# A graph network kernel: aggregation by groups of four tiles, counting by tile pairs, both with their outer loops written out

## The reference

```
out = segment_sum(hx[src] * al[:, :, None], dst, num_segments=n)   # self loops are among the edges
x = relu(out + b + x)          # first round; the second adds x and the original rows, with no relu
```

## Time and profile before

| | |
|---|---|
| median of 3 runs | 4544.77 us (4540.06 to 4547.14) |
| profiled execution | 4547.42 us, of which the span is 4545.9 us |
| busy in the span: PE, DVE | 2962.5 us, 2218.4 us |
| busy in the span: POOL, ACT | 977.4 us, 370.0 us |
| counting | about 231 to 837 us of the span |
| aggregation, round 0 and 1 | about 1254 to 1782 us, and 2124 to 2596 us |

### The profile page before, as it was taken

How to read it: one execution, slowest core, us unless ns; L and a number is a source line. 1 busy time by engine, 2 the same in 40 slices (tenths; PEclk the granted TensorE clock), 3 DMA queues, 4 the chain that set the end, 5 groups by cost and what they waited for, 6 DMA issues and landing times. The chain is left out here.

```text
span 4545.9 us, 68833 instructions
## 1 busy us (share of the span) xinstructions
PE 2962.5 (65%) x16813; PEld 1910.2 (42%) x16939; DVE 2218.4 (49%) x5486; ACT 370.0 (8%) x793; POOL 977.4 (21%) x985
## 2 busy tenths in 40 slices
PE   1467677563066765602777628923999999989476
PEld 1133333352054454501555426712656565656345
DVE  7465656587356664712444420065444444444463
ACT  0211111100000000000000012212000000000131
POOL 0000000076367700566774020020000000000000
PEclk9888989876589898756999959966999999999797
DMA  1200000253134411623553153223121212121101
GB/s 60 69 29 36 32 32 32 103 194 118 30 107 119 116 27 54 204 65 111 140 140 93 59 202 125 101 65 135 57 94 57 93 57 93 57 94 57 37 0 40
DMA packets 206513, 378.78 MB, mean 83 GB/s; under 512 B 35807, under 2 KB 155344, under 8 KB 203222
## 3 DMA queue, kind: packets, MB, share of 16 engines
q1 hardware_dynamic: 120090, 188.27, 11.9%
q0 software_dynamic: 50384, 139.33, 10.9%
q10 hardware_dynamic: 35968, 50.35, 3.2%
HBM read 270.37 MB, written 108.29 MB: 83 GB/s over the span
## 5 line engine op out<-in xcount | busy, mean ns | idle before, releaser
L1850 PE MATMUL hop_wide<-hop_hs,counts 128*128 128x512 bf16 x3000 | 990.9, 381 | 35.0 <-DMA hop_hs<-hop_parts 35.0
L1851 PE MATMUL hop_narrow<-hop_hs,counts 128*128 128x256 bf16 x3125 | 855.8, 274 | 170.6 <-DMA hop_hs<-hop_parts 155.5
L653 POOL DMA_INDIRECT gat_ring<-hx_rows,src_i x784 | 793.4, 1012 | 339.3 <-issue 211.2
L1850 PEld LDWEIGHTS hop_wide<-hop_hs,counts 128*128 (+1 forms) x3125 | 307.1, 98 | 577.9 <-issue 215.5
L888 PE MATMUL cnt_acc<-cnt_oh_src,cnt_oh_dst 128*128 x1764 | 407.0, 367 | 137.3 <-issue 71.5
L1241 PE MATMUL agg_acc<-agg_msg,agg_oh 128*128 x880 | 278.3, 444 | 126.4 <-DVE agg_oh L1180 125.9
L888 PEld LDWEIGHTS cnt_acc<-cnt_oh_src,cnt_oh_dst 128*128 x1764 | 180.5, 102 | 350.8 <-issue 292.6
L1851 PEld LDWEIGHTS hop_narrow<-hop_hs,counts 128*128 (+1 forms) x3125 | 307.2, 98 | 36.4
L1823 DVE TENSOR_SCALAR hop_h<-hop_narrow,all_dis 128x256 f32<-128x256 f32 x125 | 60.5, 484 | 527.2 <-PE hop_narrow L1851 527.2
L1241 PE MATMUL agg_acc<-gat_ring,agg_oh 128*128 x880 | 258.4, 417 | 89.0 <-DVE agg_oh L1177 89.0
L848 DVE TENSOR_SCALAR cnt_oh_src<-cnt_number,cnt_column 128x1600 f16 x441 | 277.6, 629 | 0.0
(11 more groups left out here) (408 smaller groups left out, 3557.6 us busy)
## 6 DMA issues: line engine op xcount, KB each, us to landing
look_part<-src_low SPq DMA_DIRECT2D x28, 896.0 KB, 4.9
hop_hs<-hop_parts POOLq DMA_DIRECT2D x25, 960.0 KB, 8.1
hop_parts<-hop_parts SPq DMA_DIRECT2D x125, 192.0 KB, 1.9
count_rows<-cnt_out SPq DMA_DIRECT2D x50, 400.0 KB, 2.4
counts<-count_rows ACTq DMA_DIRECT2D x5, 4000.0 KB, 35.2
exp_w<-in_L_ffn_w SPq DMA_DIRECT2D x16, 1024.0 KB
hop_acc<-x_gcn SPq DMA_DIRECT2D x125, 128.0 KB, 2.0
x_gcn<-hop_acc SPq DMA_DIRECT2D x125, 128.0 KB, 1.8
```

Of the source, the lines that this page charges most:

```text
L653: pool.indirect_dma_start(out=self.ring[:, t % RING, :], out_offset=None, in_=self.g.hx_rows, in_offset=bass.IndirectOffsetOnAxis(ap=self. ...
L1850: pe.matmul(wide[i][:, :], count, hs[:, t, 0:2 * D], start=(t == 0), stop=(t == NB - 1))
L1851: mm = pe.matmul(narrow[i][:, 0:D], count, hs[:, t, 2 * D:3 * D], start=(t == 0), stop=(t == NB - 1))
```

## The change

Counting goes by pairs of tiles, and the loop over windows is written out in the program, so that each window's first pair is known from the window before and each engine loads one bound. The one-hot slots become two sets (tile 0 and tile 1 of a pair), each of two slots. ACT makes the destination one-hot of tile 0 by two activations (Abs, then Relu), DVE the rest; ACT copies the four banks in one instruction, after it has made the first pair of the next window.

Aggregation goes by groups of four tiles with the loop over blocks written out: one multiplication for four tiles in round 0, and one-hots for two tiles at a time (one instruction in round 0, two in round 1). The node numbers come from a table that POOL fills once in `edge_weights`. The node's own row is scaled by ACT and added on PE by a product with the identity, which also opens the block in place of the zeros. The twelve idle products are gone. DVE finishes block b - 1 after the loop of block b, and prepares the residuals before it. The last cut-off at zero moves to ACT. The ring is freed by groups of four, and in round 1 `edge_weights` gathers up to pair 58 rather than 70.

The diff, cut to its core (most removed lines stand in the functions above):

```diff
...
+QUADS, HELD = ET // 4, RING // 4
...
+                link(nc.vector.tensor_scalar(g.window_pairs[:, :], g.window_tiles[:, :], 1, None, ALU.logical_shift_right))
+                link(nc.vector.tensor_scalar(g.tile_quads[:, :], g.tiles[:, :], 2, None, ALU.logical_shift_right))
...
-    AHEAD = ((60, 70, 70), (34, 42, 46))
+    AHEAD = ((60, 70, 70, 70), (34, 42, 46, 58))
...
             if q >= RING // 2:
-                pool.wait_ge(self.freed, after(q - RING // 2 + 1))
+                pool.wait_ge(self.freed, after(q // 2 - HELD + 1))
...
-            sp.sem_inc(self.in_order, 1)
+            if q % 2:
+                sp.sem_inc(self.in_order, 1)
...
-        oh_src = s.sb("oh_src", [P, DEPTH, HALF], F16)
-        oh_dst = s.sb("oh_dst", [P, DEPTH, P], F16)
+        oh_src = [s.sb(f"oh_src{k}", [P, 2, HALF], F16) for k in range(2)]
+        oh_dst = [s.sb(f"oh_dst{k}", [P, 2, P], F16) for k in range(2)]
+        minus_half, nodes, apart = s.sb("minus_half", [P, P]), s.sb("nodes", [P, 2, P]), s.sb("apart", [P, 2, P])
+        hot_a, numbered_a, far = s.sem("hot_a"), s.sem("numbered_a"), s.sem("far")
...
+        whole = [s.ps(f"acc{i}", (P, BANKS, 512)) for i in range(2)]
+        acc = [[whole[i][:, n, :] for n in range(BANKS)] for i in range(2)]
...
-        hot, used = s.sem("hot"), s.sem("used")
+        hot, used = ([s.sem(f"{n}{k}") for k in range(2)] for n in ("hot", "used"))
...
+        def last_pair(eng, w):
+            return eng.value_load(g.window_pairs[0:1, w + 1:w + 2], min_val=0, max_val=ET // 2 - 1)
...
+                def visit(p, w, then=None):
+                    for k in range(2):
+                        dve.wait_ge(used[k], after(p + w))
+                        if k:
+                            dve.tensor_scalar(at(oh_dst[k], (p + w) % 2), half16[:, :], at(key, 2 * p + k),
+                                              minus_first[:, w:w + 1], ALU.subtract, ALU.is_equal)
+                        dve.tensor_scalar(at(oh_src[k], (p + w) % 2), number[:, :], at(column, 2 * p + k), None,
+                                          ALU.is_equal).then_inc(hot[k], 1)
+                        if then and not k:
+                            found = then()
+                    return found if then else None
+                first = 0
+                for w in range(NW):
+                    last = visit(first, w, lambda: last_pair(dve, w))
                     with dve.If(last > first):
...
+                        with dve.Fori(first + 1, last + 1) as p:
+                            visit(p, w)
+                    first = last
...
+                act.wait_ge(ready, after(1))
+                def visit(p, w):
+                    slot = (p + w) % 2
+                    act.wait_ge(used[0], after(p + w))
+                    act.activation(at(apart, slot), nodes[:, w % 2, :], ACT.Abs, bias=at(key, 2 * p)).then_inc(far, 1)
+                    act.wait_ge(far, after(p + w + 1))
+                    act.activation(at(oh_dst[0], slot), at(apart, slot), ACT.Relu, scale=-2.0,
+                                   bias=g.ones[:, 0:1]).then_inc(hot_a, 1)
+                def evict(w):
+                    i, j = w % 2, w // 2
+                    act.wait_ge(summed[i], after(j + 1))
+                    act.wait_ge(stored[i], after(16 * j))
+                    act.activation(out[i][:, :].rearrange("p (n c) -> p n c", n=BANKS), whole[i][:, :, 0:COLS],
+                                   ACT.Copy).then_inc(read[i], 1)
+                first = 0
+                for w in range(NW):
+                    act.activation(nodes[:, w % 2, :], minus_half[:, :], ACT.Identity, bias=minus_first[:, w:w + 1]
+                                   ).then_inc(numbered_a, 1)
+                    last = last_pair(act, w)
+                    act.wait_ge(numbered_a, after(w + 1))
+                    visit(first, w)
+                    if w:
+                        evict(w - 1)
+                    with act.If(last > first):
+                        with act.Fori(first + 1, last + 1) as p:
+                            visit(p, w)
+                    first = last
+                evict(NW - 1)
...
-                pe.sem_inc(used, DEPTH - 1)
+                for k in range(2):
+                    pe.sem_inc(used[k], 1)
...
+                first = 0
+                for w in range(NW):
+                    i, j = w % 2, w // 2
+                    pe.wait_ge(read[i], after(j))
                     for n in range(BANKS):
...
                                   skip_group_check=True)
...
+                    last = last_pair(pe, w)
+                    with pe.Fori(first, last + 1) as p:
+                        for k in range(2):
+                            pe.wait_ge(hot[k], after(p + w + 1))
+                            if not k:
+                                pe.wait_ge(hot_a, after(p + w + 1))
+                            for n in range(BANKS):
+                                mm = pe.matmul(acc[i][n][:, 0:COLS], at(oh_dst[k], (p + w) % 2),
+                                               at(oh_src[k], (p + w) % 2)[:, n * COLS:(n + 1) * COLS],
+                                               start=False, stop=False, skip_group_check=True)
+                            mm.then_inc(used[k], 1)
                     for n in range(BANKS):
...
                     mm.then_inc(summed[i], 1)
...
+                    first = last
...
+                pool.iota(g.nodes[:, :], pattern=[[1, NP]], base=0, channel_multiplier=0,
+                          allow_small_or_imprecise_dtypes=True)
...
-                g.gather.on_gpsimd(pool, RING // 2)
+                g.gather.on_gpsimd(pool, g.gather.upto[3])
...
+        ring = g.gather.ring[:, :, :].rearrange("p (q k) r -> p q (k r)", k=4)
+        in_order, freed = g.gather.in_order, g.gather.freed
+        oh = [s.sb(f"oh{k}", [P, 2, P]) for k in range(2)]
+        msg = None if layer else s.sb("msg", [P, 2, 4 * R])
...
+        own = [s.sb(f"own{i}", [P, ROW]) for i in range(SLOTS3)]
+        res = [s.sb(f"res{i}", [P, len(residuals), D]) for i in range(SLOTS3)]
+        looped, y, inv = ([s.sb(f"{n}{i}", [P, w]) for i in range(2)] for n, w in (("looped", R), ("y", D), ("inv", H)))
...
+        acc = [s.ps(f"acc{i}") for i in range(2)]
...
+        def last_quad(eng, b):
+            return eng.value_load(g.tile_quads[0:1, b + 1:b + 2], min_val=0, max_val=QUADS - 1)
...
+                def make_self(b):
+                    act.wait_ge(loaded[b % SLOTS3], after(16 * n_loads * (b // SLOTS3 + 1)))
+                    if b >= 2:
+                        act.wait_ge(summed, after(b - 1))
+                    for h in range(H):
+                        cols = slice(h * (F + 1), (h + 1) * (F + 1))
+                        act.activation(looped[b % 2][:, cols], own[b % SLOTS3][:, cols], ACT.Copy,
+                                       scale=g.w_self[:, b, h:h + 1]).then_inc(self_made, 1)
...
+                    if not layer:
+                        act.activation(y[b % 2][:, :], y[b % 2][:, :], ACT.Relu).then_inc(turned_up, 1)
+                        act.wait_ge(turned_up, after(b + 1))
...
+                for b in range(NB):
+                    make_self(b)
+                    if b >= 2:
+                        store(b - 2)
+                    if b + 1 < NB:
+                        if b >= 2:
+                            act.wait_ge(self_made, after(H * (b - 1)))
+                        load(b + 1)
+                store(NB - 2)
                 store(NB - 1)
-                act.wait_ge(stored, after(16 * NB))
...
+                def visit(q, b, frees, then=None):
+                    found = None
+                    dve.wait_ge(in_order, after(q + 1))
                     if not layer:
...
                         weighted = dve.tensor_tensor(
...
+                            at(msg, (q + b) % 2).rearrange("p (k f) -> p k f", f=F + 1),
+                            at(ring, q % HELD).rearrange("p (k f) -> p k f", f=F + 1),
+                            g.w_cols[:, bass.ds(4 * q, 4), 0:H].rearrange("p k h -> p (k h)").unsqueeze(2)
+                            .to_broadcast([P, 4 * H, F + 1]), ALU.mult)
...
+                        dve.wait_ge(used[k], after(q + b))
...
-                            hot = dve.tensor_scalar(oh[k][:, :], at(nodes, b % 2), at(g.dst_f, 2 * p + k),
-                                                    at(g.w_cols, 2 * p + k)[:, 0:1], ALU.is_equal, ALU.mult)
+                            for n in range(2):
+                                tile = 4 * q + 2 * k + n
+                                hot = dve.tensor_scalar(oh[k][:, n, :], g.nodes[:, row_of(b)], at(g.dst_f, tile),
+                                                        at(g.w_cols, tile)[:, 0:1], ALU.is_equal, ALU.mult)
                         else:
-                            hot = dve.tensor_scalar(oh[k][:, :], at(nodes, b % 2), at(g.dst_f, 2 * p + k), None, ALU.is_equal)
```

(55 more changed lines are left out.)

151 lines of the change are left out of this document (25 added, 126 removed).

## The result

The changed kernel takes 4125.23 us (median of 4 runs, 4123.17 to 4126.51), beside 4544.41 us for the kernel before: ratio 0.9078, 95% interval 0.9062 to 0.9094. The forecast was 4269, with 4170 as the lower end.

A forecast was written before the change was run, and what follows sets the result against it. No engine is full and the time lies in gaps, with PE pacing counting. Counting -72, round 0 -60 and -62, round 1 -49 and -6, gathers -30, IOTA +1 sum to -278: from 4547.4 to 4269 us, range 4170 to 4400.

The forecast's parts named there:

- Rival C: Aggregation: PE stays at half clock, 1.75 us more on 244 steps, +427, kernel 4696 us; chance 0.05.
- late fetch of code: Rival: written-out code is fetched late, at most 2.95 us at all 100 borders, +295, kernel 4564 us; chance 0.04.
- so it hides: Aggregation round 1: POOL's 345 us of gathers fit in a stage of 418; under 350 they would be its floor.
- step of 1.97: Counting: each of 245 pair visits takes 1.97 us, 483 us; with borders 533 against 605, -72.
- second wait: Counting: a pair's second wait, shown in no row, taken as 0.11 us, between nothing and a loop gap of 0.35.
- lower bound for counting, 464: Counting: with gaps as short as in round 1's last block, a step is 0.28 us shorter, 464 in all, -141.
- rival B: Every gap shrinks because run-time addresses become constants: 489 steps x 0.28 = 137 us, kernel 4132; chance 0.15.
- 4.0 extra: Aggregation round 0: a border costs 4.0 us beyond its visit, against 6.5; 25 borders, -62 us.
- 4.75: Aggregation round 1: a border costs 4.75 us, against 5.0; 25 borders, -6 us.
- clock's 1.15: Aggregation round 1: 1.15 us added to each border for the clock, since PE sets the step there.
- 2.5: Aggregation round 0: a step of four tiles takes 2.5 us; 122 visits, 305 us against 365, -60.
- 2.45: Aggregation round 1: a step of four tiles takes 2.45 us; 122 visits, 299 us against 348, -49.

The follow-up runs named there:

- d_blocks_out_no_gathers: Kernel before without gathers after pair 70, with both aggregations' block loops written out on ACT, DVE and PE: 4688.26 us, ratio 0.9359, on a slow-gather chip.

## Why the prediction was wrong

**Right.** The direction, and the order of the stages by what they save. PE and DVE, not ACT, set counting's pace. `edge_weights` gave 28 for 30. No late fetch of code showed. Rival C did not occur: without gathers the clock stood at 1.00 over both rounds, and with them it fell only where PE waited for rows.

Four terms failed: counting's gap, the aggregation's borders (a clock drop in them), its steps, and "so it hides" for the gathers.

**Counting's step.** A step of 1.97 was 1.51 for eight matmuls, a whole loop gap of 0.35 and 0.11 for the second wait. No run shows the term of 1.51; in its place eight matmuls measured 1.52. The gap measured 0.21, with nothing for the second wait. That is 245 x 0.24 = 59 of the 62 us missed; the border's 1.0 measured 0.94. I had treated the gap as a constant of the loop. It is what is left of the sequencer's turn when the queued matmuls run out, and the change doubled the matmuls. My lower bound for counting, 464, was near the 471 measured, but the whole range took in only half of rival B.

**The borders of the aggregation.** "4.0 extra" measured 1.5, and "4.75" 2.0: 25 x 2.5 + 25 x 2.75 = 131 us, of which the clock's 1.15 is 29. I split DVE's stand of 2.95 into two bounds, a loop end and 1.2 for loop entry, and then charged entry and one bound (1.79) again; together they measured 0.81. By the trace the bound is loaded while the first group runs. In the kernel before, the written-out loop took 1.2 off a border of round 0 and 0.4 off one of round 1; finishing late is worth 16 us over all 50. What the rest is due to (the node's own row on ACT and PE, the node table, one bound fewer) no run takes apart.

**The clock.** 1.15 us of each border in round 1 was my estimate of what a drop to 0.50 costs, as after the pause of 1.43 us in the earlier trace rows. No run shows that term. In its place, pauses of 1.41 and 1.03 us within 5 us left the clock at 1.00, and so did every border without gathers. The length of a pause doesn't tell the cases apart, since up to 1.44 us left it at 1.00; what does, no run shows. In counting too the drops went: 111 us at 0.50 before, with pauses of up to 1.8 us, and 3 us, its first, after, with pauses of at most 0.82. The idle products alone didn't hold the clock: in `d_blocks_out_no_gathers` they are still there, PE then pauses 2.4 us, and the clock is at 0.50 behind nearly every border of round 0 (23 stretches of 3.4 us, 25 borders).

**The steps of the aggregation.** 2.5 measured 2.39 and 2.45 measured 2.11: 122 x 0.11 + 122 x 0.34 = 55 us. Round 0's step was costed by both engines, and DVE ends PE's gaps there. In round 1 I had 2.08 of matmuls, the smallest gap (0.27) and 0.1; it measured the matmuls alone, 2.11. Two things joined: the written-out loop brought a pair from 1.57 to 1.42, and a group of four took 2.11 in place of 2 x 1.42.

**Rival B, and luck.** It counted on constants in place of addresses. In counting they did nothing to the gap (0.33 with the loop over windows written out); in round 1 they are the likely reason for 0.15 a pair. Its 0.28 was a misreading that the forecast's lower bound shares: in the earlier trace rows the gap is 0.28 shorter than in the earlier trace rows, but the period, 1.41 for 1.58, only 0.17, which would have given 489 x 0.17 = 83 us and 4186. The steps saved 59 + 55 = 114 us more than the forecast, and B had neither the borders (131) nor the gathers (97 the other way). That its 4132 came within 7 us is luck.

**The gathers: "so it hides".** It doesn't. The prediction named the floor ("if the stage came under 350") and then costed the stage at 418, by steps and borders that were too long. Without gathers the stages would take 341 and 320; with them 397 and 361, so 56 + 41 = 97 us came back. In round 0 I had no floor at all, though POOL had 252 x 1.25 = 315 us there too. And while PE waits for rows, its clock falls (0.75 from 1378 us on). The longer multiplication added 118 x 0.49 = 58, and 315 + 58 = 373 is just the time from POOL's first gather of the stage (1126.9) to its last (1500.1).

The sum: 62 in counting, and 131 + 55 - 97 = 89 in the aggregation, make 151; the forecast missed by 144.

## What to carry to other kernels

Before a loop gap is multiplied by a count of steps, ask what it would be if more work were queued ahead of it: run the engine's own streaming time (0.172 a matmul here) beside the period, and see whether the difference goes as the step grows (0.50, 0.35 and 0.00 us at 4, 8 and 16 matmuls here). And when an edit's total comes out as forecast, look in the trace where the time went: the 65 us of the written-out block loop matched the theory, but half of them lay in the steps and not in the borders. When a stage shrinks, compute the floor of every engine in it anew, those that were hidden by 150 us too, and with the instructions that now run beside them: a merged instruction that runs longer holds its neighbour longer (a held gather lost 0.19 us before, and 0.49 after). A transfer moved out of an exposed place is only saved if the stage that takes it isn't bound by the same queue (moving 24 gathers back shifted the whole by 10 us or less here, though `edge_weights` grew by 27 to 30).
